# The first two steps of an attention and mixture-of-experts kernel: split input load, filler products on TensorE, reordered copies and vector work

## The reference

```
sa, ca, ga, sb, cb, gb = mod                      # ga, gb: magnitude at least 0.25
h = layernorm(x) * (1 + ca) + sa
q, k, v = split(h @ W_in.T)                       # 16 heads of 16 channels
xq, xk = clip(q / 4, -1, 1), clip(k / 4, -1, 1)
Tq, Tk = Chebyshev polynomials of order 0..10 (weights beta nonzero for orders 1..5)
num = sum_n beta_n * Tq_n * cumsum_over_tokens(Tk_n * v)
den = sum_n beta_n * sum(Tq_n) * cumsum_over_tokens(sum(Tk_n))
x = x + ga * ((num / (den + 1e-7)) @ W_out.T)
h = layernorm(x) * (1 + cb) + sb
shared = silu(h @ sW1 + sb1) @ sW2 + sb2
routed = sum over the top 2 of 8 experts of sqrt(softplus(logit)) * (silu(h @ rW1 + rb1) @ rW2 + rb2)
x = x + gb * (shared + routed)
```

## Time and profile before

| what | value |
|---|---|
| median of 3 runs | 894.32 us |
| profiled execution, its own time | 893.84 us |
| span of that execution, first to last instruction | 892.1 us |
| PE (TensorE matmul) busy | 849.3 us, 95% |
| DVE (VectorE) busy | 800.8 us, 90% |
| ACT (ScalarE) busy | 487.2 us, 55% |
| POOL (GpSimd) busy | 283.4 us, 32% |
| mean granted TensorE clock | 0.977 of full |

### The profile page before, as it was taken

How to read it: one execution, slowest core, us unless ns; L and a number is a source line. 1 busy time by engine, 2 the same in 40 slices (tenths; PEclk the granted TensorE clock), 3 DMA queues, 4 the chain that set the end, 5 groups by cost and what they waited for, 6 DMA issues and landing times.

```text
span 892.1 us, 14249 instructions
## 1 busy us (share of the span) xinstructions
PE 849.3 (95%) x4377; PEld 645.0 (72%) x4377; DVE 800.8 (90%) x1367; ACT 487.2 (55%) x874; POOL 283.4 (32%) x351
## 2 busy tenths in 40 slices
PE   5796969999999999999999999999999999989998
PEld 5555646886868687786868687786868688666787
DVE  3799979999999999999999999999999999989643
ACT  5744566565656566564656556565656656351320
POOL 1131241423424151423424062333425053242330
PEclk9886979999999999999999999999999999999999
DMA  9022225364535445364544536464444535443623
GB/s 327 4 56 76 48 61 161 73 173 96 143 87 105 132 92 176 72 172 91 135 90 87 156 75 175 90 168 77 113 126 76 147 72 148 97 121 71 159 74 81
DMA packets 51612, 99.98 MB, mean 112 GB/s; under 512 B 5395, under 2 KB 34142, under 8 KB 49510
## 3 DMA queue, kind: packets, MB, share of 16 engines
q1 hardware_dynamic: 36388, 66.14, 23.4%
q0 software_dynamic: 14688, 32.51, 21.6%
q10 hardware_dynamic: 482, 0.74, 0.2%
HBM read 57.68 MB, written 17.06 MB: 84 GB/s over the span
## 4 chain that ended last, share of the span: by engine, by line
PE 81%; DVE 9%; DMA 3%; issue 2%; ACT 2%; POOL 1%; SPq 0%; DVEq 0%; POOLq 0%
PE ring L1494 34%; PE acc L1613 25%; PE tr L1547 8%; PE tr L1571 6%; PE tr L1485 3%; DVE feat L1061 2%; DMA feat<-inv_rows 2%; PE misc L1520 2%; PE acc L1602 1%; ACT ntok L454 1%; PE misc L1528 1%; DVE feat L1082 1%; DMA inv_rows<-denom 1%; PE acc L1625 1%; DVE feat L1086 1%
## 5 line engine op out<-in xcount | busy, mean ns | idle before, releaser
L1613 PE MATMUL acc<-w,hid 128*128 128x256 f32 x1128 | 261.0, 379 | 0.5 <-DVE hid L1240 0.5
L1613 PEld LDWEIGHTS acc<-w,hid 128*128 128x128 f32 x1128 | 213.1, 189 | 34.3 <-DVE hid L1240 1.1
L864 ACT ACTIVATE hid<-ring,b1row 128x512 f32<-128x512 f32 x144 | 96.8, 682 | 162.3 <-PE ring L1494 160.8
L689 POOL DMA_DIRECT2D feat<-feat x47 | 42.7, 908 | 344.0 <-DVE feat L1082 210.2
L812 ACT ACTIVATE feat<-ring,bqkv 128x512 f32<-128x512 f32 x96 | 65.8, 687 | 85.2 <-PE ring L1494 85.2
L1494 PE MATMUL ring<-n2H,w1H 128*128 128x512 f32 x288 | 107.9, 456 | 0.0
L1061 DVE TENSOR_TENSOR_SCAN feat<-zero,carry,feat 128x512 f32<-128x512 f32 x80 | 97.2, 1267 | 0.0
L1061 DVE TENSOR_TENSOR_SCAN feat<-zero,feat 128x512 f32<-128x512 f32 x80 | 92.4, 1204 | 0.0
L1240 DVE TENSOR_TENSOR hid<-hid,cfw 128x512 f32<-128x512 f32 x128 | 85.1, 679 | 8.1 <-DMA cfw<-cf_rows 5.5
L1494 PE MATMUL ring<-n2H,w1L 128*128 128x512 f32 x288 | 90.5, 395 | 0.0
L1494 PE MATMUL ring<-n2L,w1H 128*128 128x512 f32 x288 | 90.5, 395 | 0.0
(11 more groups left out here) (169 smaller groups left out, 1408.1 us busy)
## 6 DMA issues: line engine op xcount, KB each, us to landing
feat<-feat POOLq DMA_DIRECT2D x47, 512.0 KB, 4.6
...
```

The costliest lines, as they stand in the source:

```text
L689: g.dma_start(f(into), f(of), accum_op=ALU.add).then_inc(added[n], 16)
L864: a.activation(hid[:, e], ring[bank][:, :], ACT.Silu, bias=b1row[:, e:e + 1]).then_inc(ring_copied, 1)
L1613: last = mm(acc[t // 2][:, t % 2], hid[:, e, t * P:(t + 1) * P], w2[:, e], start=False, stop=(e == E), skip_group_check=True)
```

## The change

Every edit lies in the setup, the prologue, step 0 or step 1; the code of all later steps orders its instructions as before.

1. W_in is loaded in two halves, with chunk 0 of x between them. TensorE waits for each half on its own.
2. `keep_running(n)` issues n products of constants on TensorE (f32, 384 columns) into a bank of `acc`, which nothing reads. It stands at the end of the setup block (1), in step 0 ahead of the projection (2) and ahead of `project_out` (2), and in step 1 ahead of `project_out` (11).
3. In the prologue ScalarE copies q0 ahead of the third square of k.
4. `bias_products` is split: the products of two experts stand ahead of the denominators of step 0, the rest behind.
5. In step 0 VectorE inverts the denominators between the clips of k and q, not behind both.
6. `second_bias_rows` moves from the end of step 0 to step 1, ahead of `divide`. The temporary space moves to slots 6 to 8 of `hid`, so that step 1 may write slots 0 to 5.

```diff
--- before.py
+++ after.py
@@ -164,6 +164,7 @@
         cfR = sb("cfR", [SPL, CT], f32r)
         cfT = sb("cfT", [P // 2, CT])
         cfw = sb("cfw", [P, NW, CT])
+        AHEAD = 6
         hid = sb("hid", [P, NE, CT])
 
 
@@ -193,7 +194,7 @@
         assert used[0] <= NW * CT
 
 
-        late, at_late = hid.rearrange("p g t -> p (g t)"), [0]
+        late, at_late = hid[:, AHEAD:NE].rearrange("p g t -> p (g t)"), [0]
 
         def tmp_late(n):
             v = late[:, at_late[0]:at_late[0] + n]
@@ -206,7 +207,7 @@
         b1_rows, b1T, eb = tmp_late(HID), tmp_late(NE), tmp_late(1)
         rtF = tmp_late(KD * QS).rearrange("p (k e) -> p k e", k=KD)
         r2f, r2h, r2l = tmp_late(D), tmp_late(D), tmp_late(D)
-        assert at_late[0] <= NE * CT and NT * D == KD * HID * (E // 2)
+        assert at_late[0] <= (NE - AHEAD) * CT and NT * D == KD * HID * (E // 2)
 
 
         tr = [ctx.enter_context(nc.psum_tensor(f"tr{k}", [P, CT], f32)) for k in range(2)]
@@ -287,7 +288,6 @@
                 (B, 0, AFTER_LAST), (B, 1, some("ffn"))]
 
 
-        AHEAD = 6
         RING = ["f6", "f7", "f8", "k0", "k1", "q0", "q1", "e0", "e1", "e2", "v0", "v1", "e3", "e4", "e5"]
         RING_STAGE = {"e": "second", "f": "ffn"}
         USES = len(RING)
@@ -328,6 +328,7 @@
 
         CARRY_COPIES = ((0, 2, 1), (3, 2, 3), (2, 1, 4))
         LAST_TILES = (0, 2, 1, 3)
+        KEEP = 3 * P
         HALVES = ["k0", "k1", "q0", "q1", "v0", "v1"]
         CHUNK0 = {u: (k, k % 2) for k, u in enumerate(HALVES)}
 
@@ -463,8 +464,9 @@
 
 
         in_c, in_wmod_b = sem("in_c"), sem("in_wmod_b")
-        in_win, in_wout, in_small, in_const, in_wmod, in_w1, in_w2, in_r2, in_gates = (
-            sem(f"in_{n}") for n in ("win", "wout", "small", "const", "wmod", "w1", "w2", "r2", "gate_rows"))
+        in_win = [sem(f"in_win{half}") for half in range(2)]
+        in_wout, in_small, in_const, in_wmod, in_w1, in_w2, in_r2, in_gates = (
+            sem(f"in_{n}") for n in ("wout", "small", "const", "wmod", "w1", "w2", "r2", "gate_rows"))
         s_tr = sem("setup_transposed")
         s_silu, s_scT = sem("setup_silu"), sem("setup_scT")
         s_hi, s_mods, s_modps, s_gps, s_g1, s_g2 = (sem(f"setup_{n}") for n in (
@@ -474,12 +476,20 @@
         s_bias, s_b1T, s_r2 = sem("setup_bias_products"), sem("setup_b1T"), sem("setup_r2")
         s_winT, s_rtT, s_wo, s_pow = sem("setup_winT"), sem("setup_rtT"), sem("setup_wo"), sem("setup_exponents")
 
+        def keep_running(n):
+
+            idle_bank = acc[1].rearrange("p g d -> p (g d)")
+            for _ in range(n):
+                nc.tensor.matmul(idle_bank[:, 0:KEEP], ident, const[:, 0:KEEP], start=True, stop=True)
+
         with nc.Block() as block:
             @block.sync
             def _(sp):
-                sp.dma_start(win_rows, w_in_d.rearrange("(m p) d -> p m d", p=P)).then_inc(in_win, 16)
-                for p in range(CB):
-                    load(sp, 0, p)
+                w_in_rows = w_in_d.rearrange("(m p) d -> p m d", p=P)
+                sp.dma_start(win_rows[:, 0:3], w_in_rows[:, 0:3]).then_inc(in_win[0], 16)
+                load(sp, 0, 0)
+                sp.dma_start(win_rows[:, 3:6], w_in_rows[:, 3:6]).then_inc(in_win[1], 16)
+                load(sp, 0, 1)
                 sp.dma_start(w1f[0], sw1_d.rearrange("(k p) h -> p k h", p=P)).then_inc(in_w1, 16)
                 sp.dma_start(w1f_routed.rearrange("p e k h -> p (e k) h"),
                              rw1_d.rearrange("e (k p) h -> p (e k) h", p=P)).then_inc(in_w1, 16)
@@ -552,8 +562,8 @@
                 for k in range(KD):
                     last = nc.tensor.transpose(tr[0][:, k * B:(k + 1) * B], silu_c[0:B, k * P:(k + 1) * P], ident[0:B, 0:B])
                 last.then_inc(s_tr, 1)
-                pe.wait_ge(in_win, 16)
                 for m in range(6):
+                    pe.wait_ge(in_win[m // 3], 16)
                     if m >= 2:
                         pe.wait_ge(s_winT, m - 1)
                     for k in range(KD):
@@ -575,6 +585,7 @@
                     nc.tensor.transpose(ring[1][:, 64 + k * E:64 + (k + 1) * E], rt_rows[0:E, k * P:(k + 1) * P],
                                         ident[0:E, 0:E])
                 nc.tensor.transpose(ring[1][:, 128:128 + NE], b1_rows[0:NE, :], ident[0:NE, 0:NE]).then_inc(s_tr, 1)
+                keep_running(1)
 
 
         block = ctx.enter_context(nc.Block())
@@ -969,10 +980,11 @@
             act.wait_ge(s_bqkv, 1)
             copy_qkv(0, 0, CHUNK0, "k0")
             copy_qkv(0, 0, CHUNK0, "k1")
-            for which in range(3):
-                square(0, 0, 0, which)
+            square(0, 0, 0, 0)
+            square(0, 0, 0, 1)
             act.wait_ge(s_bqkv, 2)
             copy_qkv(0, 0, CHUNK0, "q0")
+            square(0, 0, 0, 2)
             copy_qkv(0, 0, CHUNK0, "q1")
             act.wait_ge(s_bqkv, 3)
             copy_qkv(0, 0, CHUNK0, "v0")
@@ -1324,13 +1336,14 @@
                     den_products(i, p)
                 if second:
                     logit_ranks(*prev)
-                if attn_ and not first:
+                if first:
+                    clip(*nxt, use, 0)
+                if attn_:
                     invert(i, p)
+                if qkv and not first:
+                    clip(*nxt, use, 0)
                 if qkv:
-                    clip(*nxt, use, 0)
                     clip(*nxt, use, 1)
-                if first:
-                    invert(i, p)
                 if not last_attention:
                     expert(5)
                 else:
@@ -1359,6 +1372,8 @@
                     finish_first_numerator()
                 elif attn_:
                     finish_numerator(i, p)
+                if isinstance(i, int) and number(i, p) == 1:
+                    second_bias_rows()
                 if attn_:
                     divide(i, p)
                 if ffn:
@@ -1452,7 +1467,6 @@
             for i, p, st in FIRST:
                 step(i, p, st)
                 if number(i, p) == 0:
-                    second_bias_rows()
                     biases_out()
                     dve.wait_ge(late_biases, 2)
                     dve.wait_ge(late_weights, 2)
@@ -1640,7 +1654,8 @@
                         elif e == E:
                             last_experts_by_tile(*exp)
 
-                if isinstance(i, int) and number(i, p) == 0:
+                first = isinstance(i, int) and number(i, p) == 0
+                if first:
                     late_products_of_mods()
                 if ffn:
                     expert_up(*exp, use, 6)
@@ -1653,6 +1668,9 @@
                 expert(0)
                 if second:
                     transposes(1, *prev, behind_norm=qkv)
+                if first:
+                    pe.wait_ge(s_wo, 2)
+                    keep_running(2)
                 if qkv:
                     for half in HALVES[:3]:
                         project(*nxt, use, half)
@@ -1671,6 +1689,8 @@
                 if qkv:
                     project(*nxt, use, "v0")
                     project(*nxt, use, "v1")
+                if first:
+                    first_bias_products(range(2))
                 if attn_:
                     denominators(i, p)
                 expert(4)
@@ -1678,8 +1698,13 @@
                 expert(6)
                 expert(7)
                 expert(8)
-                if isinstance(i, int) and number(i, p) == 0:
-                    bias_products()
+                if first:
+                    first_bias_products(range(2, NE))
+                    logit_bias_products()
+                    pe.wait_ge(s_wo, 2)
+                    keep_running(2)
+                elif isinstance(i, int) and number(i, p) == 1:
+                    keep_running(11)
                 if attn_:
                     project_out(i, p)
                 if second:
@@ -1770,13 +1795,16 @@
                             last = mm(misc[:, o:o + B], wmod_b[k][:, at:at + P], scT[:, k], start=(k == 0), stop=(k == KD - 1))
                 last.then_inc(s_late_mods, 1)
 
-            def bias_products():
+            def first_bias_products(experts):
 
                 pe.wait_ge(s_scaled, 1)
                 pe.wait_ge(in_w1, 32)
-                for e in range(NE):
+                for e in experts:
                     for k in range(KD):
                         mm(cfb[:, e * B:(e + 1) * B], w1f[e][:, k], mods[:, 2, k], start=(k == 0), stop=(k == KD - 1))
+
+            def logit_bias_products():
+
                 for k in range(KD):
                     last = mm(cfb[0:E, 128:128 + B], rtF[:, k, 0:E], mods[:, 2, k], start=(k == 0), stop=(k == KD - 1))
                 last.then_inc(late_products, 1)
```

## The result

The changed kernel took 889.56 us (median of 6 runs, 888.16 to 890.79) beside 894.38 us for the kernel before (6 runs, 892.60 to 896.08). The ratio is 0.9944, with a 95% interval from 0.9929 to 0.9960: 5.0 us or 0.56% faster, against 6.1 us forecast. The profiled execution took 889.10 us (span 887.4) for 893.84 us (span 892.1). (Three executions in the experiments stand far above all others of their kernel, one of e9 with 1433.9 us, one of e4 with 903.7 us and one of the kernel before beside e12 with 4460 us, and the ratios leave them out.)

The account below looks back on a forecast made before the run. TensorE's clock and work bound the steady part, so earlier gains stay. 0.35 + 0.65 + 0.7 + 0.6 + 2.1 - 0.6 + 0 + 2.3 = 6.1 us gave a median of 888.2 us, range 884.7 to 891.4.

Parts of the forecast that it names:

- Setup: End of the setup block: the second block's transposes start at 16.25 instead of 16.61 us, gain 0.35 us.
- Clock in the prologue: Prologue: the filler may raise TensorE's clock sooner for k0 and k1; gain 0.65 us, between 0 and 1.3.
- V: Prologue: v1 ends sooner because q0 is copied ahead of a square; gain 0.7 us, bounds 0.4 and 0.9.
- Inverse between the clips: Step 0: the inverse, and the division waiting for its transfer, come sooner; gain 0.6 us, bounds 0.3 and 0.9.
- project_out of step 0: End of step 0: two fillers raise the clock during this projection, which takes 4.5 us; gain 2.1, bounds 2.7 and 1.3.
- the prediction's sign: Step 0: project_out was to take between 3.9 and 5.3 us, with the residual right behind it.
- Start of step 1: Start of step 1: the clock falls again and may rise later than before; cost 0.6 us, bounds 0 and 1.25.
- The four instructions: Step 1 ahead of divide: VectorE's bias rows, about 1.6 us, fit its 2.00 us wait; cost 0, bounds 0 and 1.4.
- The rival of the lock: Step 1: the four VectorE instructions wait out GpSimd's splits, divide 1.0 to 1.4 us late; 889.3 us, chance 0.08.
- Eleven fillers: Step 1: they fill TensorE's gap, so project_out takes 3.62 instead of 5.91 us; gain 2.3, bounds 1.5 and 2.6.
- the rival in which products of constants don't hold the clock: Step 1: the clock falls after 4 fillers, project_out starts 3 us late and slow; 895.6 us, chance 0.04.
- The rival "swallowed": Step 2: a load or store that doesn't shift bounds it, and the time stays at 894.3 us; chance 0.05.

Follow-up runs that it names:

- e9: The kernel of e8 without the product of constants at the end of the setup; ratio 0.9916 to the kernel before.
- e4: The changed kernel without the product of constants in the setup and the two ahead of step 0's first projections; 892.26 us, ratio 0.9982.
- e12: The kernel of e9 with step 0's products of constants spread among the bias products and two more behind the last; 887.39 us, ratio 0.9923.
- e1: The changed kernel run again, unaltered; 891.26 us, ratio 0.9973 to the kernel before.
- e2: The changed kernel without any product of constants, all reordering kept; 892.16 us, ratio 0.9980.
- e8: The kernel of e5 with eight small loads of second-layer biases moved from the setup into the second block; 887.55 us, ratio 0.9935.
- e7: The changed kernel without the eleven products of constants ahead of step 1's projection; 891.96 us, ratio 0.9977.
- e5: The changed kernel with GpSimd's output transfer in the last attention step waiting until the routing weights' rows are written; 887.12 us, ratio 0.9920.
- e3: The kernel before with only products of constants added, 2 and 11 ahead of project_out in steps 0 and 1; 896.32 us, ratio 1.0026.
- e11: The kernel of e5 with VectorE's second bias rows back at the end of step 0; 890.25 us, ratio 0.9942.
- e6: The kernel before with the same added wait as e5; 893.72 us, ratio 0.9993.

## Why the prediction was right, and where it was not

The forecast was 888.2 us, the measured median 889.56. The sum was 6.1 us. The trace has 7.7 us ahead of the tail, and 3.0 us taken back in it. e1's median, 891.26 us, lies only just inside the range that ends at 891.4.

*Setup: wrong.* Forecast a gain of 0.35, measured a loss of 0.23. I took TensorE for the last at the meeting, and asked of its filler alone. In the kernel after it ended at 16.36, but SyncE's own issuing of loads ended at 16.28 and the block began at 16.84; in e2, without the filler, it began at 16.75, 0.55 us behind SyncE as here (0.56). Where TensorE was last, in e8, it began 0.3 us behind it, which would have given 16.66 here. The rows of SyncE's queue were in the trace of before and I did not read them. e8 and e9 show the three limits one after the other. ScalarE did come sooner, by 1.2 us (13.05 for 14.24), and it was worth nothing.

*Clock in the prologue and V: right in sum.* Forecast 0.65 + 0.7. `weigh` gained 1.10 with the setup's -0.23, so both together gave 1.33, as much as the two forecast terms, 1.35; they can be told apart only in part. The twelve matmuls for k0 and k1 took 4.76 us, 0.52 less than in the earlier trace rows, since the clock rose at 24.2 instead of 25.1. The rest, 0.8, is V's: VectorE has no idle time at 33.66 where it had 1.52. But the clock's part is no effect of the filler: in e4, without it, the clock rose at 25.3, and in e12, also without, at 25.1, but in e9, without it as well, at 22.1. From the start of the block to the rise it took 6.6 us (e1) to 9.6 us (e7) in different executions. The Trainium skill, "TensorE: Matmul & The Clock Gate", Part 1 on the warm-up, says that the number of slow matmuls differs from run to run of the same kernel; the traces of e1 and of the changed kernel, one and the same program, agree (6.6 and 7.4 us from the block's start to the rise).

*Inverse between the clips: right.* From `weigh` to the end of the inversion it gained 0.6 us (it ends at 63.54 for 65.25, 1.71 sooner, less the 1.10). No run isolates it.

*project_out of step 0: the right mechanism, undersized here.* Forecast 2.1 of a possible 2.7; measured 2.9 (3.72 for 6.62). The rise came at its start, the best case. In e4, e5 and e7 the same two products gave 5.47, 5.90 and 6.15 us, in e1, e3, e8, e9 and e11 3.72 again, and without them it took 6.62, 6.14 (e6) and 5.73 us (e2). The nine with them average 4.4 us, close to the 4.5 forecast, and the three without 6.2, so the gain averages 1.7 us where 2.1 was forecast. No execution lay between 3.9 and 5.3 us, as the prediction's sign wanted: the rise came in time or late. That the gain needs the bias rows moved away was the prediction's condition, and e3 and e11 show it: without the move 3.5 of 3.6 us are lost in the one, and 3.3 us in the other.

*Start of step 1: wrong.* Forecast a cost of 0.6, measured none. The clock was low from 78.8 to 85.7 us, but VectorE's rows there have no idle time and all stages shift by the same 4.6 us (`L1132` at 113.85 for 118.47).

*The four instructions: right, and a bonus.* They took 1.55 us from 114.98 on, by the sign asked of them (under 2 us), and cost nothing; the division even came 5.17 us sooner than before where its forerunner came 4.62 us sooner. The rival of the lock did not come about for VectorE. At the old place the two-input instruction stood beside GpSimd's 2.35 us product and took 2.47 us in e11; at the new place it took 0.42. GpSimd's last splits were the ones that lengthened:

```profile
116.27 1.03 POOL L733 TENSOR_TENSOR split<-part,pool_c 128x32 f32<-128x32 bf16 x2
117.38 0.68 POOL L733 TENSOR_TENSOR split<-split,pool_c 128x96 f32<-128x96 f32 x1
```

These are the kernel after's. In e11 the same two take 0.56 and 0.35 us, where `divide` begins only as they end; here they ran beside `divide` (116.52 to 117.86). Beside the four instructions themselves a split of 0.24 us took at most 0.30. The rule that the forecast quoted, of the Trainium skill, "SBUF — State Buffer", that the one who comes second waits out the other's whole instruction, agrees with these places: beside instructions of 0.2 to 0.5 us that is little for either.

*Eleven fillers: right.* Forecast 2.3, measured 2.19 (3.72 for 5.91). All eleven took 7.26 us, 0.66 each. They ended at 116.96, inside `divide` and 0.95 us before `project_out`, and the rival in which products of constants don't hold the clock is refuted: in e7, without them, it fell at 118.9.

*The end of the kernel: not foreseen.* The rival "swallowed" looked for something that doesn't shift, in step 2, and gave it 0.05. It was right in kind, wrong in place and size: what doesn't shift rigidly is the order of two transfers in the last attention step, which hung on a late sum of orders. The step of the argument that failed is "every microsecond won or lost before it stays in the total, because all engines shift together". It held to the last projection, and no further. The sign "1.00 without a gap from about 111 to the end" failed with it, at 788.8 and 836.6 us. e5 and e6 show that the order is the cause of the waits; the fall of the clock behind it is the larger part, and why it came in three executions of five is open. The median came within 1.4 us of the forecast because a gain larger than forecast and a loss not foreseen nearly cancelled. That was luck.
